# Layer 0 of a two-layer transformer: how the negated row maxima are scaled, and the order of the exponentials

## The reference, cut to what matters

```python
x = _layernorm(x + L0_attn(x))        # latent attention, causal, 16 heads
x = _layernorm(x + L0_ffn(x))         # 16 experts, 2 per token
x = _layernorm(x + L1_attn(x))        # grouped attention, position bias, capped scores
x = _layernorm(x + L1_ffn(x))         # binarised weight
```

```python
q = rmsnorm(x @ Wq_a, q_norm_w) @ Wq_b                # 128 + 64 (rotated) per head
kv = rmsnorm(x @ Wkv_a, kv_norm_w) @ Wkv_b
scores = einsum('bqhd,bkhd->bhqk', qf, kf) / sqrt(192)
scores = where(mask, scores, min)                     # causal
p = softmax(scores)
o = einsum('bhqk,bkhd->bqhd', p, v) ; o @ Wo
```

## Time and profile before

| | us |
|---|---|
| median of 3 runs | 527.75 (527.48 to 530.24) |
| the profiled execution, its own time | 526.13 |
| its span, first to last instruction | 524.3 |
| PE busy | 489.1 (93%) |
| DVE busy | 378.5 (72%) |
| ACT busy | 350.3 (67%) |
| POOL busy | 316.4 (60%) |
| layer 0's steps, first to last row maximum | 32.7 to 168.4 |

### The profile page before, as it was taken

One profiled execution on the slowest core, in us unless ns is written; L12 is line 12 of the kernel. 1 busy time (PEld: TensorE's weight loads), 2 busy tenths in 40 slices (PEclk: granted clock), 3 DMA queues, 4 the chain that ended last, 5 costly groups with the idle time before them and its releaser, 6 DMA issues.

```text
span 524.3 us, 10836 instructions
## 1 busy us (share of the span) xinstructions
PE 489.1 (93%) x3625; PEld 431.1 (82%) x3648; DVE 378.5 (72%) x833; ACT 350.3 (67%) x791; POOL 316.4 (60%) x319
## 2 busy tenths in 40 slices
PE   8899999999999997799975999999999999999994
PEld 7678888888888786588854888999999999999884
DVE  4798888878874266655555899879757985588556
ACT  5758888877877755344432788768766876676663
POOL 5759898889886136345560688776554564465330
PEclk9999999999999999799996999999999999999999
DMA  7939999950000492345575000000000000000001
GB/s 260 397 101 385 316 316 322 329 181 1 1 2 1 151 376 83 103 132 163 163 261 191 2 0 1 1 1 3 1 1 0 1 2 2 1 0 1 2 22 60
DMA packets 17761, 56.84 MB, mean 108 GB/s; under 512 B 2628, under 2 KB 12362, under 8 KB 15914
## 3 DMA queue, kind: packets, MB, share of 16 engines
q1 hardware_dynamic: 14960, 49.81, 28.0%
q0 software_dynamic: 2752, 6.40, 3.7%
HBM read 49.19 MB, written 28.45 MB: 148 GB/s over the span
## 4 chain that ended last, share of the span: by engine, by line
PE 60%; POOL 9%; DVE 8%; issue 8%; ACT 7%; DMA 6%; SPq 1%; POOLq 0%; ACTq 0%; DVEq 0%
PE bank L450 10%; PE bank L452 9%; PE bank L451 9%; PE bank L1007 5%; PE bank L515 4%; DMA wvo_raw<-in_wvo 4%; POOL qT L2030 3%; ACT probs L1138 3%; PE bank L1024 2%; PE bank L751 2%; PE bank L736 2%; PE bank L738 2%; PE bank L737 2%; POOL probs L2038 2%; PE bank L627 2%
## 5 line engine op out<-in xcount | busy, mean ns | idle before, releaser
L1138 ACT ACTIVATE probs<-bank,neg_max,q_scale 128x256 f32<-128x256 f32 (+1 forms) x128 | 63.8, 509 | 22.0 <-DVE neg_max L1822 22.0
L2080 POOL TENSOR_TENSOR exps<-exps,tables 128x256 f32<-128x256 f32 x32 | 25.7, 802 | 70.8 <-ACT exps L1253 70.7
L2038 POOL TENSOR_TENSOR probs<-probs,inv_sum 128x512 f32<-128x512 f32 x64 | 51.7, 829 | 21.8 <-DVE inv_sum L1830 21.7
L1253 ACT ACTIVATE exps<-bank 128x768 f32<-128x768 f32 x32 | 25.9, 809 | 37.8 <-PE bank L718 37.7
L2176 POOL DMA_INDIRECT y_rows<-y_slot,dest x31 | 29.8, 961 | 30.3 <-issue 19.0
L1635 DVE TENSOR_TENSOR q_lo<-q_sum,q_hi 128x512 fp32r<-128x512 f32 x32 | 29.0, 906 | 26.0 <-ACT q_hi L1207 25.7
L2067 POOL TENSOR_TENSOR swapped<-swapped,tables 128x512 f32<-128x512 f32 x32 | 43.2, 1352 | 5.9 <-ACT swapped L1174 5.7
L1808 DVE TENSOR_TENSOR swapped<-bank,tables 32x512 f32<-32x512 f32 x64 | 44.4, 693 | 1.4
L2030 POOL TENSOR_TENSOR qT<-qT,swapped 128x512 f32<-128x512 f32 x32 | 41.0, 1283 | 6.2 <-DVE swapped L1808 6.2
L450 PE MATMUL bank<-x,wq_hi 128*128 128x256 f32 x128 | 38.5, 301 | 0.1
L450 PE MATMUL bank<-wo_hi,c_hi 128*128 128x256 f32 x128 | 37.5, 293 | 0.0
(11 more groups left out here) (291 smaller groups left out, 1827.5 us busy)
## 6 DMA issues: line engine op xcount, KB each, us to landing
slots<-in_c_unused SPq DMA_DIRECT2D x20, 1036.0 KB, 35.8
gu_all<-in_gate_up SPq DMA_DIRECT2D x4, 1024.0 KB, 8.5
xg<-slots SPq DMA_DIRECT2D x31, 129.5 KB
wvo_raw<-in_wvo SPq DMA_DIRECT2D x1, 2560.0 KB, 19.0
dn_all<-in_down SPq DMA_DIRECT2D x1, 2048.0 KB, 7.7
wq_full<-in_Wq SPq DMA_DIRECT2D x1, 2048.0 KB
wo_raw<-in_Wo SPq DMA_DIRECT2D x1, 2048.0 KB
wqk_raw<-in_wqk SPq DMA_DIRECT2D x1, 1536.0 KB, 9.9
```

The lines of the kernel that those rows point to most:

```text
L1138: ins = act.activation(probs[:, par, h, c0:c1], bank[:, 2 * par + h, c0:c1], ACT.Exp, bias=neg_max[:, par, i:i + 1], scale=q_scale[:, b, t ...
L2038: ins = pool.tensor_tensor(some, some, inv, ALU.mult)
```

## The change

The one product for four scaled maxima becomes two, each for one tile of both heads, with the scale read as a scalar per partition (a column of `q_minus`) in place of a broadcast operand. Each waits for its own maximum and signals `max_ready` by itself. The exponentials, which ran head by head (first tile, second tile, first tile, second tile), now run tile by tile (first tile of both heads, then second tile of both), and ScalarE waits for each tile's signal.

```diff
@@ act_attention0
-                act.wait_ge(at["max_ready"], n + 1)
                 if lag(2):
                     act.wait_ge(at["probsT_done"], n - 1)
-                for h in range(2):
-                    for tile, c0, c1 in ((0, 0, T), (1, T, T + P)):
+                for tile, c0, c1 in ((0, 0, T), (1, T, T + P)):
+                    act.wait_ge(at["max_ready"], 2 * n + tile + 1)
+                    for h in range(2):
                         i = 2 * tile + h
                         ins = act.activation(probs[:, par, h, c0:c1], bank[:, 2 * par + h, c0:c1], ACT.Exp,
@@ dve_attention0
-                dve.wait_ge(at["max_step"], 2 * n + 2)
-                dve.tensor_tensor(neg_max[:, par, :].rearrange("p (t h) -> p t h", t=2),
-                                  row_max[:, par, :].rearrange("p (t h) -> p t h", t=2),
-                                  q_minus[:, b, :].unsqueeze(2).broadcast_to([P, 2, 2]),
-                                  ALU.mult).then_inc(at["max_ready"], 1)
+                for t in range(2):
+                    dve.wait_ge(at["max_step"], 2 * n + 1 + t)
+                    dve.tensor_scalar(neg_max[:, par, 2 * t:2 * t + 2], row_max[:, par, 2 * t:2 * t + 2],
+                                      q_minus[:, b, t:t + 1], None, ALU.mult).then_inc(at["max_ready"], 1)
```

## The result

| us | before | after |
|---|---|---|
| median (4 runs each) | 528.02 (527.48 to 530.24) | 535.26 (534.44 to 538.24) |
| ratio, 95% interval | | 1.015 (1.0114 to 1.0186) |
| span of the profiled execution | 524.3 | 532.6 |
| first to last row maximum of layer 0 | 135.6 | 143.8 |

The account below looks back on a forecast made before the run. TensorE was taken to set layer 0's steps. Losses of 6.8 us in six groups and 1.1 in the first four steps, 7.9, made 526.13 into 534.0; with the median 1.6 higher, 535.6 us, range 526 to 540.

Parts of the forecast that it names:

- What bounds it: Layer 0's attention: TensorE alone sets 4.17 us a step; the exponentials' 22.0 us of waiting can't be collected.
- Step (a): VectorE's scaling: one operation of 0.16 removed, two of 0.21 each added, first starting about 0.1 earlier; without GpSimd, nothing.
- Step (b): ScalarE's exponentials reordered: the same four instructions and one more wait, nearly always met; 0.
- Step (c): Earlier first tile: nothing on the path, since the reciprocal stands behind VectorE's cosine and sine products; at most a tenth.
- Step (d): VectorE asks twice for the exclusion with GpSimd; the second scale waits one whole GpSimd instruction, 0.73 to 1.29 us.
- The sum: Layer 0's steps: 1.13 us lost a group, 6.8 over six groups, plus 1.1 in the first four steps: 7.9.
- Rival 1: The second scale slips through before GpSimd's next instruction; 528.2 us, chance 0.16.
- Rival 2: A two-element VectorE operation takes no part in the exclusion with GpSimd at all; 525.3 us, chance 0.14.
- Rival 3: Holds mostly meet short instructions; only 0.59 of each last-batch chain is left, six times, 3.5 us; 531.2 us, chance 0.20.
- What would show it: Second scale ending 0.02 behind GpSimd, query waits near 1 us for sines, last-batch stalls staying, exponentials waiting 5 to 10 less.

Follow-up runs that it names:

- e1: Kernel before with only the exponentials reordered tile by tile, one product and one signal kept; 526.7 us, ratio 0.9992.
- e3: Kernel before, one product kept, with the row maxima written to four free columns of a scores bank in PSUM; 526.6 us, ratio 0.9977.
- e4: Changed kernel with exponentials in the old order behind both signals and the row maxima in PSUM; 528.4 us, ratio 0.9991.
- e2: Changed kernel's two scales alone, with the exponentials in the old order and behind both signals; 537.8 us, ratio 1.0178.
- e5: Changed kernel with each tensor_scalar replaced by a two-column tensor_tensor, scale as broadcast operand, operands in SBUF; 527.0 us, ratio 0.9990.
- e6: Changed kernel with the constant -1/sqrt(192) in place of the scalar per partition in both scales; 527.5 us, ratio 0.9995.
- e10: Changed kernel with the scalar per partition in the first scale only, the constant in the second; 527.4 us, ratio 0.9993.
- e11: Changed kernel with the constant in the first scale, the scalar per partition in the second only; 536.8 us, ratio 1.0197.
- e13: Kernel before with GpSimd's subtraction of the last batch of each pair moved behind the sine addition; 541.2 us, ratio 1.0252.

## Why the prediction was right, point by point

- **What bounds it.** TensorE sets the steps, and VectorE's and GpSimd's chains enter only where their slack runs out: e1, e3 and e4 move scales and exponentials by up to 0.6 us and the time by 0.1 to 0.2%. The 22.0 us of waiting exponentials was no prize: e3 freed the product entirely and gained 1.3 us of the steps.
- **Step (a), the price of the operations.** Estimated 0.21 each, the first 0.1 earlier. Measured 216 ns (e4), the first at R + 0.94 where the product had been at R + 1.06. Right.
- **Step (b), the order of the exponentials: 0.** e1: right. **Step (c):** nothing in the runs speaks against it; e2 doesn't tell what the early first tile is worth once the second scale is late. In the changed kernel the second tile's exponentials wait at most 0.13 us for the late scale, so the loss goes by the cosine and sine products that stand behind it on VectorE, as forecast.
- **Step (d), the exclusion.** That a tiny tensor_scalar takes part, that the first goes in at the end of GpSimd's instruction, and that the second loses a whole instruction because of its fetch: each seen, the last by e5, e6, e10 and e11 (for 20 of the 30 second scales that were held; in the other 10 steps the first had not been held, and there a pair without the fetch loses the second too). The estimate behind it was two distances, 0.07 and 0.13, on either side of GpSimd's 0.08. The runs fit that order of the three; they show neither the figures nor the asking itself. The Trainium skill, SBUF — State Buffer, section Who interferes with whom, says that one of the two engines gets what they share for its whole instruction and the other is blocked. The trace agrees: a held scale ends 0.02 behind the GpSimd instruction it met. But the prediction's sentence that VectorE and GpSimd exclude each other is too wide: the reciprocal of this stage (four columns, SBUF to SBUF) keeps 177 to 180 ns in all 32 steps of the kernel before, also in the eight in which it lies inside a GpSimd instruction.
- **The sum.** Group of four steps: 18.53 forecast, 135.07 - 116.59 = 18.48 measured, 17.40 before. The total is right, and in part by luck, since its terms are not those forecast. In steps 10, 14, 18 and so on the matmuls wait 0.74 to 0.76 us for the sines, where 0.95 was forecast; before the contexts they idle 0.42 to 0.49 once in a group, where 0.90 was to stay; in its place each of the other two steps takes 4.29 in place of 4.17. Steps 4 to 28: +6.8 forecast, +6.1 measured, 0.3 of the difference from the size of the group and 0.4 from the first group, which takes 18.1 and not 18.5. First four steps: +1.1 forecast, +1.8 measured: in steps 0 and 2 the second scale met an instruction of 1.27, I had counted one such hold. Last four: 0 and +0.2. Together 7.9 against 8.2; the two misses cancel in part. The medians of the runs lie 7.2 apart. That the forecast of 535.6 is only 0.3 from the measured 535.3 owes something to scatter as well.
- **Rival 1** (slipping through) is what e5, e6 and e10 do in most steps; it gave 528.2, and 527.0 to 527.5 was measured. **Rival 2** (no exclusion) is wrong for scales in SBUF: GpSimd held 30 of the 32 second ones of the changed kernel. Moving the maxima to PSUM makes it true, and there its price was too high: forecast 525.3, measured 526.6 (e3). The term that was mis-sized is the 1.2 us for the first four steps; e3 took 17.3 us for them and before 17.6. **Rival 3** (only the last-batch chains are left) isn't what ran: the waits for the sines are there in every group.
- **What would show it.** The waits on the sines and the durations came as said. Wrong was that TensorE's last-batch stalls would stay: they were 0.42 to 0.48 and 0.81 to 0.86 in turn and are 0.42 to 0.49 now. Wrong was also that the exponentials would wait less: 24.4 us from 34 to 183 us, 22.0 before. They start earlier behind the row maxima in most steps, but the steps have become 8 us longer, and ScalarE spends that time waiting.

## What to carry to other kernels

Where VectorE and GpSimd both work in SBUF, count how often a chain on VectorE asks for what they share, and what each ask does before it reads: here a short operation right behind a held one went in with it in most steps (69 of 75 in e5, e6 and e10), and one with a scalar per partition let GpSimd's next instruction, 0.6 to 1.3 us long, in between in all 40 (the changed kernel and e11). A small operand that one VectorE operation writes and the next reads can lie in PSUM, which took the asking away here. And a wait in a list is worth what hangs on its end: read the slack of the next consumer (here 0.29 us) before counting it as a gain or a move as free.

## What the runs showed of the hardware

- One fetched scalar costs 0.06 us (154 ns bare without it, 219 with it, e10). In the second scale in place of the first it moved the kernel by 9.4 us (e10 to e11): the second scale was held in 30 steps in place of 9.
- A VectorE instruction that starts 0.02 us before a GpSimd one in the timeline can still be held by it for its whole 1.27 us (step 18 of e11): starts in the profile don't say whose turn it is.
- With the tensor operand in PSUM an operation of 4 or 2 columns was never held, though its scalar per partition or its second operand came from SBUF: 161 to 164 ns (e3) and 210 to 220 (e4) over all steps.
- tensor_reduce takes 700 ns into PSUM and 692 into SBUF (512 elements).
- Not every VectorE instruction in SBUF is held by GpSimd: in the kernel before the reciprocal of four columns took 177 to 180 ns in all 32 steps, the product of four columns 163 to 723.
- In e13 TensorE's granted clock was 0.50 from 75.6 to 78.0, behind an idle time of 2.02 us, and 1.00 from 70 to 75; a matmul of 0.36 us took 0.55 there.
